# All pooled products of batch 1 ahead of group 0's x3 transposes, the gate weights' low halves on VectorE, Wsoma's split and the late tiles reordered

## The reference

```
x = x + pooled(x)          # tanh scores, masked softmax over 2048 rows, weighted sum of rows, / count
x = x + du_dt(x)           # zX*(left + right - 2x) + zY*(above + below - 2x) + zR*x*(1-x)
x = x + adapter(x)         # h = x + relu(x Wd + bd) Wu + bu;  layernorm(h) * g + b
x = x + block(x):
    ctx    = ema(x, alpha_ctx)                       # along time
    wg     = sigmoid([x, ctx] Wg^T + bg);  gated = x * wg
    h1     = gelu(x Wn1^T + bn1);  mod = 0.5 + sigmoid(h1 Wn2^T + bn2)   # two traces
    traces = ema(gated * mod_d, tau_d);  temporal = sum_d traces_d * softmax(blend)_d
    gate   = sigmoid(temporal Wtemp^T + btemp)
    soma   = gelu(x Wsoma^T + bsoma)
    out    = layernorm((soma * gate) Wout^T) * gamma + beta
```

## Time and profile before

| | us |
|---|---|
| runs (3) | 724.22, 727.25, 729.0; median 727.25 |
| profiled execution, its own time | 727.25 |
| its span, first to last instruction | 725.3 |
| PE busy | 669.2 (92%) |
| DVE busy | 552.6 (76%) |
| ACT busy | 357.3 (49%) |
| POOL busy | 200.6 (28%) |
| mean granted TensorE clock | 0.972 of full speed |

### The profile page before, as it was taken

One profiled execution on the slowest core, in us unless ns is written; L12 is line 12 of the kernel. 1 busy time (PEld: TensorE's weight loads), 2 busy tenths in 40 slices (PEclk: granted clock), 3 DMA queues, 4 the chain that ended last, 5 costly groups with the idle time before them and its releaser, 6 DMA issues.

```text
span 725.3 us, 8102 instructions
## 1 busy us (share of the span) xinstructions
PE 669.2 (92%) x2808; PEld 490.6 (68%) x2808; DVE 552.6 (76%) x767; ACT 357.3 (49%) x725; POOL 200.6 (28%) x265
## 2 busy tenths in 40 slices
PE   4969989375999999999999999999999999999996
PEld 1545444254867786778677877777877788787884
DVE  3665886643998898879878997797788758775965
ACT  1143378315458435843583458345734653465235
POOL 5003463603353322322232224222420310031001
PEclk9989999597999999999999999999999999999999
DMA  7995899699414561466045704560466050014001
GB/s 209 304 381 171 171 225 303 196 235 352 130 23 88 133 104 26 87 143 111 8 88 145 117 4 85 145 116 16 88 116 116 1 117 1 0 19 98 1 1 58
DMA packets 51654, 85.77 MB, mean 118 GB/s; under 512 B 8464, under 2 KB 10512, under 8 KB 51614
## 3 DMA queue, kind: packets, MB, share of 16 engines
q0 software_dynamic: 16896, 33.56, 28.2%
q1 hardware_dynamic: 31230, 51.69, 20.3%
q10 hardware_dynamic: 3488, 0.01, 0.3%
HBM read 63.22 MB, written 22.04 MB: 118 GB/s over the span
## 4 chain that ended last, share of the span: by engine, by line
PE 73%; DVE 9%; DMA 7%; ACT 4%; POOL 3%; issue 2%; SPq 1%; POOLq 0%; DVEq 0%; ACTq 0%
PE bank L1100 19%; PE bank L1101 19%; PE bank L1102 19%; PE bank L1001 3%; PE bank L1140 3%; PE bank L1156 3%; DMA ws_l_f<-in_wsoma 3%; PE bank L1203 2%; DMA xr<-beside_scratch 2%; PE bank L1130 1%; DMA beside_scratch<-xb 1%; DMA xts<-in_xT 1%; DVE tr L1623 1%; PE bank L1096 1%; PE bank L1165 1%
## 5 line engine op out<-in xcount | busy, mean ns | idle before, releaser
L1615 DVE TENSOR_TENSOR_SCAN tr<-alpha,carry,tr 128x512 f32<-128x512 f32 x48 | 60.9, 1310 | 0.0
L1609 DVE SCALAR_TENSOR_TENSOR tr<-wgb,blend_w,mod 128x512 f32<-128x512 f32 x64 | 46.0, 750 | 12.6 <-ACT mod L809 11.7
L1100 PE MATMUL bank<-xh,wg_l 128*128 128x512 f32 x128 | 52.6, 411 | 0.0
L1100 PE MATMUL bank<-th,wg_l 128*128 128x512 f32 x128 | 51.8, 405 | 0.0
L1101 PE MATMUL bank<-xl,wg_h 128*128 128x512 f32 x128 | 50.8, 397 | 0.0
L1101 PE MATMUL bank<-tl,wg_h 128*128 128x512 f32 x128 | 50.4, 394 | 0.0
L1102 PE MATMUL bank<-xh,wg_h 128*128 128x512 f32 x128 | 50.2, 392 | 0.0
L1102 PE MATMUL bank<-th,wg_h 128*128 128x512 f32 x128 | 49.7, 388 | 0.0
L615 POOL TENSOR_TENSOR rs_a<-ss_a,consts 128x1 f32<-128x1 f32 x32 | 17.2, 536 | 113.2 <-ACT hb L784 113.0
L824 ACT ACTIVATE carry<-tr 128x2 f32<-128x2 f32 x32 | 6.5, 204 | 75.9 <-DVE tr L1615 75.9
L1490 DVE SCALAR_TENSOR_TENSOR xb<-bank,rnorm,xb 128x512 f32<-128x512 f32 x32 | 23.1, 746 | 22.1 <-PE bank L1097 22.0
(11 more groups left out here) (254 smaller groups left out, 2015.4 us busy)
## 6 DMA issues: line engine op xcount, KB each, us to landing
x2b<-beside_scratch POOLq DMA_DIRECT2D x12, 1024.0 KB, 9.0
xr<-rows_scratch POOLq DMA_DIRECT2D x10, 1024.0 KB, 10.3
xb<-in_x SPq DMA_DIRECT2D x8, 1024.0 KB, 14.5
result<-xr SPq DMA_DIRECT2D x7, 1024.0 KB, 4.3
x2b<-rows_scratch POOLq DMA_DIRECT2D x6, 1024.0 KB, 10.1
x_scratch<-xb SPq DMA_DIRECT2D x5, 1024.0 KB, 15.0
beside_scratch<-xts SPq DMA_DIRECT2D x5, 1024.0 KB, 18.6
late_y<-x_scratch SPq DMA_DIRECT2D x20, 256.0 KB, 2.7
```

The lines of the kernel that those rows point to most:

```text
L1100: pe.matmul(acc, wl, xh_, start=start, stop=False)
L1609: ve.scalar_tensor_tensor(t[:, d], w, blend_w[:, d, k:k + 1], mod[:, d], ALU.mult, ALU.mult).then_inc(tr_in, 1)
L1615: ve.tensor_tensor_scan(t[:, d], alpha[:, 1 + d:2 + d].broadcast_to([P, GN]), t[:, d], 0.0 if first else carry[:, k, 1 + d:2 + d], ALU.mul ...
```

## The change

On TensorE pooled(1, 10) to (1, 15) go ahead of x3_transposes(0). On VectorE the x1 tiles of batch 1 are interleaved with group 0's ln_weigh and ln_apply, and three weight_low (Wn1 and the two halves of Wg) come over from GpSimd. On ScalarE scale_beside(5) and (6) go ahead of x3_evict(0), with all three slots of xts in turn, and Wsoma's split goes from ahead of group 0 to behind sigmoid_gate(0, 1); on GpSimd its low half goes behind add_before(2). On SP store_x1(6) goes ahead of Wsoma's load, store_x1(7) and store_beside(7) go ahead of Wout's. TensorE's soma_in(0, 0) waits for one weight2_low instead of two. In every group with late tiles, tile 0's work on ScalarE and VectorE goes behind the last product, tile 1's behind the whole of x3_evict and x3_lo, and late_channels for tile 0 behind the four rstd of the adapter.

```diff
 def scaled_of(n):
-return x1_of(n) if n < HEAD_BLOCKS else as_tiles(xts[:, n % 2])
+return x1_of(n) if n < HEAD_BLOCKS else as_tiles(xts[:, n % 3])
 
...
         store_beside(n)
+    store_x1(6)
     sp.wait_ge(x1_out[4], 16)
...
     sp.dma_start(ws_st[:], chunks(wsoma)).then_inc(w2_in[0], 16)
-    store_x1(6)
     store_beside(6)
+    store_x1(7)
+    store_beside(7)
     sp.wait_ge(pool_mm, B * NT)
     sp.dma_start(wo_st[:], chunks(wout)).then_inc(w2_in[2], 16)
-    store_x1(7)
-    store_beside(7)
     sp.wait_ge(x1_out[6], 16)
...
 
-    def weight_low(i, hi, lo, stage):
-        po.wait_ge(w_hi, i + 1)
-        po.tensor_tensor(lo, stage, f32(hi), ALU.subtract).then_inc(w_lo, 1)
-
     def weight2_low(n, hi, lo, stage):
...
     channels(2)
-    weight_low(0, wn1_h[:], wn1_l[:], wn1_st[:])
     add_before(1)
     add_after(1)
-    weight_low(1, wg_h[:, 0:KE], wg_l[:, 0:KE], wg_st[:, 0:KE])
     for c in range(GT):
         rstd(ln_ss, ss_a, EPSILON, rs_a, c, ln_p, ln_rs, c)
-    weight_low(2, wg_h[:, KE:], wg_l[:, KE:], wg_st[:, KE:])
     add_shift(0)
     add_up_bias(2)
-    weight2_low(1, ws_h[:], ws_l[:], ws_st[:])
     for g in range(GROUPS):
...
             if g == 0:
+                weight2_low(1, ws_h[:], ws_l[:], ws_st[:])
                 weight2_low(2, wo_h[:], wo_l[:], wo_st[:])
...
             weight2_low(3, wt_h[:], wt_l[:], wt_st[:])
-        if late:
-            late_channels(g + 3, 0)
         if g < LAST:
...
                 rstd(ln_ss, ss_a, EPSILON, rs_a, GT * (g + 1) + c, ln_p, ln_rs, c)
+            if late:
+                late_channels(g + 3, 0)
             add_shift(g + 1)
...
             act.wait_ge(x1_done, GT * (n + 1))
-        if n >= HEAD_BLOCKS + 2:
-            beside_landed(act, (n - 2) // NG, (n - 2) % NG)
+        if n == HEAD_BLOCKS + 2:
+            act.wait_ge(local_done, HEAD_BLOCKS)
+        elif n > HEAD_BLOCKS + 2:
+            beside_landed(act, (n - 3) // NG, (n - 3) % NG)
         act.activation(scaled_of(n), x1_of(n), ACT.Identity, scale=coef[:, ZY, b:b + 1])\
...
         if q == HEAD_BLOCKS:
-            act.wait_ge(local_done, HEAD_BLOCKS)
+            beside_landed(act, 1, 1)
         else:
...
 
-    def x3_evict(q, chosen=ks):
+    def x3_evict(q):
         xh = x3_pair(q)[0]
-        for k in chosen:
+        for k in ks:
             act.wait_ge(x3T_mm, KE * q + k + 1)
...
     wg_hi(1, wg_h[:, KE:], wg_st[:, KE:])
+    scale_beside(5)
+    scale_beside(6)
     act.wait_ge(x1_out[3], 16)
     x3_evict(0)
-    scale_beside(5)
-    scale_beside(6)
-    weight_hi(0, ws_h[:], ws_st[:])
     scale_beside(7)
...
         sigmoid_gate(g, 1)
+        if g == 0:
+            weight_hi(0, ws_h[:], ws_st[:])
         trace_hi(g, 0)
...
                 product_hi(g, k - 1)
-            if k == 1 and late:
-                late_mix(g + 3, 0)
         product_hi(g, KE - 1)
+        if late:
+            late_mix(g + 3, 0)
         if adapted:
-            x3_evict(g + 1, (0, 1))
-            if late:
-                late_mix(g + 3, 1)
-            x3_evict(g + 1, (2, 3))
+            x3_evict(g + 1)
+        if late:
+            late_mix(g + 3, 1)
         for c in range(GT):
...
         if g == 0 and k == 0:
-            pe.wait_ge(w2_lo, 2)
+            pe.wait_ge(w2_lo, 1)
         if k == 0:
...
     up(0)
-    for c in range(6, 10):
+    for c in range(6, NT):
         pooled(1, c)
     x3_transposes(0)
-    for c in range(10, NT):
-        pooled(1, c)
     for g in range(GROUPS):
...
 
+    def weight_low(i, hi, lo, stage):
+        ve.wait_ge(w_hi, i + 1)
+        ve.tensor_tensor(lo, stage, f32(hi), ALU.subtract).then_inc(w_lo, 1)
+
     def late_by_local(q, c):
...
 
-    def x3_lo(q, chosen=ks):
+    def x3_lo(q):
         xh, xl = x3_pair(q)
-        for k in chosen:
+        for k in ks:
             ve.wait_ge(x3T_hi, KE * q + k + 1)
...
     normalise(1)
+    weight_low(0, wn1_h[:], wn1_l[:], wn1_st[:])
     x1(1, 0)
...
     x1(1, 3)
+    weight_low(1, wg_h[:, 0:KE], wg_l[:, 0:KE], wg_st[:, 0:KE])
     x1(1, 4)
...
     x1(1, 6)
-    for c in range(GT):
-        ln_weigh(0, c)
+    ln_weigh(0, 0)
+    ln_weigh(0, 1)
     x1(1, 7)
-    for c in range(GT):
-        ln_apply(0, c)
+    ln_weigh(0, 2)
+    ln_weigh(0, 3)
     x1(1, 8)
+    ln_apply(0, 0)
     x1(1, 9)
+    ln_apply(0, 1)
     x1(1, 10)
+    ln_apply(0, 2)
     x1(1, 11)
+    ln_apply(0, 3)
+    for c in range(12, NT):
+        x1(1, c)
+    weight_low(2, wg_h[:, KE:], wg_l[:, KE:], wg_st[:, KE:])
     x3_lo(0)
-    x1(1, 12)
-    x1(1, 13)
-    x1(1, 14)
-    x1(1, 15)
     assert n["p"] == S_PARAMS, n["p"]
...
             product_lo(g, k - 1)
-            if late and k == 1:
-                late_by_local(g + 3, 0)
-                late_stencil(g + 3, 0)
         product_lo(g, KE - 1)
+        if late:
+            late_by_local(g + 3, 0)
+            late_stencil(g + 3, 0)
         if adapted:
-            x3_lo(g + 1, (0, 1))
-            if late:
-                late_by_local(g + 3, 1)
-                late_stencil(g + 3, 1)
-            x3_lo(g + 1, (2, 3))
+            x3_lo(g + 1)
+        if late:
+            late_by_local(g + 3, 1)
+            late_stencil(g + 3, 1)
         for c in range(GT):
...
                 late_by_local(g + 3, 2)

```

## The result

| | before | after |
|---|---|---|
| median (runs) | 726.35 us (4 runs, 724.22 to 729.0) | 717.11 us (4 runs, 716.07 to 717.6) |
| ratio after to before | | 0.987, 95% interval 0.985 to 0.989 |
| profiled execution: its time, span | 727.25, 725.3 | 717.48, 715.7 |
| mean granted TensorE clock | 0.972 | 0.983 |

The kernel is 1.3% faster; the forecast of 711 us was 6 us too low.

The account below looks back on a forecast made before the run. TensorE was taken to be the bound from M to the end, with Wout's landing limiting group 0's gain. Span 725.3 - 11.3 (group 0) - 4.5 (late tiles) = 709.5, forecast 711 us as executed; range 700 to 721.

Parts of the forecast that it names:

- M: Start of group 0's first MOD product on TensorE: claimed to move from 170.53 to 149, two waits (12.1, 9.5 us) gone.
- Wout: Landing of Wout's weight load in group 0: claimed at 176.7, four us later than before, ScalarE waiting some 11 us.
- The account: Sum of DMA transfers up to Wout's landing: 2.55 us per SP transfer, 6.4 per accumulation; 25.6 of 27.7 us before.
- Group 0: From Wout to group 0's end: last trace_lo claimed at 202.1, TensorE from there 11.3 us earlier.
- The first rival: Wout not late, group 0 bound by VectorE's chain: needed product at 195.5, 18 us gained, 704 us; 17%.
- The late tiles: TensorE's waits for product_lo(3) in groups 0 to 3: claimed gone with the new order, 4.5 us won.
- its last rival: Late tiles too late for the next group's logits, loads of 8.5 us: 26 us lost, 742 us; 5%.

Follow-up runs that it names:

- the head: Everything in the change but the late tiles' new order: the changed kernel with late tiles in their old order, against the kernel before; 711.15 us, 0.9809.

## Why the prediction was right in its range and wrong in two of its steps

**M.** Right: 151.2 against 149, both waits of the earlier trace rows gone, the DMA engines busy throughout from 140 to 150 (share 0.98, then 1.10). The gate weights' part measured 4.3 us alone, the order 6.0.

**Wout.** This step failed: "Sum: 137.5 + 27.7 + 5.1 + 6.4 = 176.7". Wout landed at 169.2, and ScalarE came to it at 170.54 without a wait instead of waiting 11 us; it came there 5 us later than the 165 of the prediction, held up with VectorE's scans. The term that was wrong is the last, add_before(2)'s 6.4 us ahead of Wout. The account laid the accumulations in full ahead of the plain transfers: Wsoma landed at 149.8, not 160, while add_up_bias(2), issued 2.2 us behind it, landed only at 163, so that add_before(2), which waits for that, was issued at 163.37, with Wout nearly through. The rest of the sum fits this trace: x1(5), issued at 129.14, landed at 138.4 where the prediction had 139.6, and its sum without add_before(2), 170.3, less these 1.2 us is 169.1.

```profile
x_scratch<-xb SPq DMA_DIRECT2D x1, 1024.0 KB, 9.3
```

The account also followed SP's queue alone and passed over the third subtraction, Wn1's. In the kernel before GpSimd had waited for Wn1's high half and run its subtraction ahead of add_before(1):

```profile
104.98 2.58 POOL L598 TENSOR_TENSOR wn_l<-wn_l_f,wn_h 128x512 fp32r<-128x512 f32 x1 [3.38 <-ACT wn_h L863]
107.50 1.32 POOL L588 DMA_DIRECT2D xr<-beside_scratch  x1
```

Now add_before(1) goes at 102.07, not at 107.50, and add_after(1) at 117.55, not at 121.46 (it now waits for a store of SP's and no longer for add_before(1) to land). With Wn1 put back Wout is at 174.9, with add_before(2) well ahead of it again; by which of the transfers in between that comes about is not shown. That the account of the kernel before closed proved less than it seemed: it fixes the sum of the transfers, not who goes first.

The Trainium skill (DMA: Bandwidth & Descriptors, "Issuing engines are not separate DMA queues") has them interleave. The trace agrees with that: Wsoma (138.52 to 149.8) and the accumulation issued at 139.87 (landed at 155.0) were under way together, and neither held the other back in full. It was the forecast that, having cited it, still put one queue ahead of the other.

**Group 0.** The first rival's mechanism (17%), a chain of VectorE with three meetings with GpSimd, is what happened: the product that needs the last trace_lo starts at 196.26, against its 195.5, and its sign, Wout landing before 170, came too. But it priced this as TensorE's bound; in the trace TensorE loses only 1.7 + 2.5 us to it and is itself the bound otherwise. Taking all three meetings away gave some 2.5 us, at the edge of what the runs can tell; and the 704 that went with this rival counted 4.5 us won on the late tiles, where some 5 were lost.

The Trainium skill (SBUF — State Buffer, "Who interferes with whom") has GpSimd share VectorE's second pair of ports, locked against each other. The traces agree: 7.10, 4.91 and 3.31 us beside GpSimd, 2.33 and 0.68 without.

**The late tiles.** This term had the wrong sign: 4.5 us were to be won, and 4.6 (on the kernel before) to 6 (on the head; 4.5 by the ratios) were lost. What it said of product_lo was right: 5.7 us of waits, where the prediction had counted 4.5, became 0.9. What it left out of the forecast it had in its last rival (5%): the load beside add_shift, whose sign, waits at logits, came in groups 1 to 5. That was mis-sized: two loads of 8.5 us in each group were to cost 26 us; one, of 7.8 us in group 0, cost 10.7 in five groups.

**The sum.** The two errors nearly cancel: the head gave 13.9 in place of 11.3, the late order took about 5 in place of giving 4.5. 711 - 2.6 + 9.5 = 718, against 717.1. So the time came out inside the range, but by luck in these two, not by the steps that led to 711.

## What to carry to other kernels

Ask of each moved step what it will run beside: here a wait of 1.3 us was cured by an order that put a 256 KB load behind a 1 MB accumulation and cost twice as much, and leaving the order and adding one wait was worth 6 us more. When transfers of two queues are summed to forecast a landing, give it both with and without the other queue's ahead, and carry both through to a time: the prediction had written 170.3 beside its 176.7, and 169.2 is what came. Follow every queue that feeds the engines back to the first thing that the change removes. A subtraction that two engines can do may be cheaper on the one that it would otherwise block: here 2.3 us on VectorE against 2.6 to 4.8 us of VectorE's time lost beside GpSimd's 4.6 to 5.2. Off the bound that gives little: some 2.5 us for the three in group 0, 4.3 to 6.0 for the gate weights' two ahead of M.

## What the runs showed of the hardware that was not expected

- A VectorE scan over two SBUF tiles is held up by GpSimd's subtraction like a two-tile addition: two scans took 7.10 us beside a subtraction of 5.16, and 2.33 alone.
- 1 MB for Wout landed at 169.2 when issued at 148.28 and at 168.8 when issued at 162.81, so 20.9 and 6.0 us from issue to landing for the same transfer.
- A plain load of 256 KB right behind an accumulating transfer of 1 MB took 7.8 us in place of 2.7 to 2.9.
- The same head put M anywhere from 149.3 to 152.9 in single executions of six kernels that differ only behind it.
- Behind an idle time of 2.68 us in group 2 the granted clock of TensorE was 0.76 for 5 us in one execution, which cost 1.6 us; behind one of 2.93 us in group 1 of the same execution it stayed at 1.00.
